# Cross-attention of a six-layer block on Trainium2: a new hand-written order for the short-context loop

## What is computed

```python
xn  = layer_norm(x, gamma)
ctx = layer_norm(context, ctx_gamma)          # context: 16 x 1601 x 512
q = (xn @ Wq) in 16 heads of 64, times 64**-0.5
k, v = split(ctx @ Wkv)                       # one key head and one value head for all 16 query heads
sim = where(mask == 0, -inf, q @ k.T)
out = softmax(sim) @ v ; out = out @ Wout + silu(gate) * a @ Wff2
```

## Time and profile before

| | before |
|---|---|
| median of 3 runs | 1497.53 us |
| the profiled execution | 1495.54 us |
| its span, first to last instruction | 1493.7 us |
| mean granted TensorE clock | 0.954 of full speed |
| PE busy | 1287.0 us (86%) |
| DVE busy | 916.6 us (61%) |
| ACT busy | 585.0 us (39%) |
| POOL busy | 502.7 us (34%) |
| chain that ended last, by engine | PE 63%, DVE 22%, issue 5%, ACT 4%, DMA 2% |

### The profile page before, as it was taken

How to read it: one execution, slowest core, us unless ns; L and a number is a source line. 1 busy time by engine, 2 the same in 40 slices (tenths; PEclk the granted TensorE clock), 3 DMA queues, 4 the chain that set the end, 5 groups by cost and what they waited for, 6 DMA issues and landing times.

```text
span 1493.7 us, 29148 instructions
## 1 busy us (share of the span) xinstructions
PE 1287.0 (86%) x11410; PEld 734.2 (49%) x11518; DVE 916.6 (61%) x2053; ACT 585.0 (39%) x1165; POOL 502.7 (34%) x424
## 2 busy tenths in 40 slices
PE   6857777787879999999998787989897998879998
PEld 2435555555664444444444445444444455555554
DVE  7768877776673333300367777485998366575761
ACT  3535676777763222231032416142314234233430
POOL 3002200000009555444225410054690039996300
PEclk9978999999999999999999997999999999769999
DMA  6223233221102211463100100031320001110000
GB/s 186 70 82 111 73 102 105 84 64 39 46 2 85 84 57 43 97 197 100 57 29 16 44 30 29 12 101 58 113 92 29 1 1 59 58 58 1 1 22 36
DMA packets 57474, 92.37 MB, mean 62 GB/s; under 512 B 14449, under 2 KB 14961, under 8 KB 57345
## 3 DMA queue, kind: packets, MB, share of 16 engines
q1 hardware_dynamic: 49728, 75.55, 16.3%
q10 hardware_dynamic: 5696, 8.76, 2.0%
q0 software_dynamic: 1920, 6.29, 1.3%
HBM read 88.49 MB, written 2.10 MB: 61 GB/s over the span
## 4 chain that ended last, share of the span: by engine, by line
PE 63%; DVE 22%; issue 5%; ACT 4%; DMA 2%; DVEq 0%; ACTq 0%; SPq 0%
PE psum L669 41%; PE psum L999 7%; PE psum L1323 4%; DVE big L2299 3%; DVE big L2305 2%; PE psum L678 2%; DMA ybuf<-in_ctx_dram 2%; PE psum L905 1%; DVE big L2280 1%; PE psum L1011 1%; DVE stats L2241 1%; PE psum L1311 1%; ACT big L1445 1%; PE psum L923 1%; DVE big L2512 1%
## 5 line engine op out<-in xcount | busy, mean ns | idle before, releaser
L3076 POOL TENSOR_TENSOR ring_hi<-stage,small 128x512 bf16<-128x512 f32 x128 | 140.8, 1100 | 635.0 <-DVE big L2324 396.8
L669 PE MATMUL psum<-y_mem,ring_hi 128*128 128x512 bf16 x867 | 263.3, 383 | 9.3 <-issue 4.3
L669 PE MATMUL psum<-ring_hi,y_mem 128*128 128x512 bf16 x551 | 168.2, 391 | 6.2 <-DVE ring_lo L2638 3.3
L669 PE MATMUL psum<-y_mem,ring_lo 128*128 128x512 bf16 x440 | 168.4, 383 | 0.3
L3079 POOL TENSOR_TENSOR ring_lo<-stage,ring_hi 128x512 bf16<-128x512 f32 x128 | 154.5, 1207 | 10.0
L669 PEld LDWEIGHTS psum<-y_mem,ring_hi 128*128 (+1 forms) x896 | 87.0, 99 | 108.9 <-issue 10.0
L1445 ACT ACTIVATE big<-psum 100x512 bf16<-100x512 f32 (+3 forms) x208 | 112.0, 554 | 55.5 <-PE psum L678 45.7
L669 PE MATMUL psum<-ring_lo,y_mem 128*128 128x512 bf16 x347 | 117.0, 390 | 3.6 <-issue 1.7
L669 PEld LDWEIGHTS psum<-ring_hi,y_mem 128*128 128x128 bf16 x576 | 57.5, 100 | 74.4 <-issue 11.9
L2305 DVE TENSOR_TENSOR big<-psum,big 100x512 bf16<-100x512 f32 x128 | 87.0, 680 | 8.2 <-ACT big L1445 6.9
L2409 DVE TENSOR_TENSOR side<-psum,ybuf 128x512 f32<-128x512 f32 x32 | 22.1, 691 | 110.3 <-ACT ybuf L1672 110.3
(11 more groups left out here) (273 smaller groups left out, 2783.8 us busy)
## 6 DMA issues: line engine op xcount, KB each, us to landing
ybuf<-in_ctx_dram SPq DMA_DIRECT2D x64, 200.0 KB
big<-in_ctx_dram SPq DMA_DIRECT2D x64, 200.0 KB
stage<-in_L_xattn_Wff_dram SPq DMA_DIRECT2D x12, 1024.0 KB, 5.4
ybuf<-in_L_ffn_W_fc_dram ACTq DMA_DIRECT2D x16, 256.0 KB, 2.8
ybuf<-in_L_ffn_W_proj_dram ACTq DMA_DIRECT2D x16, 256.0 KB, 2.8
stage<-in_L_ffn_W_fc_dram SPq DMA_DIRECT2D x4, 1024.0 KB, 5.2
stage<-in_L_ffn_W_proj_dram SPq DMA_DIRECT2D x4, 1024.0 KB, 5.1
stage<-in_L_xattn_Wout_dram SPq DMA_DIRECT2D x3, 1024.0 KB, 5.2
```

The source lines that it names most:

```text
L669: ins = pe.matmul(bank, l, r, start=n == 0, stop=n == len(passes) - 1)
L3076: pool.tensor_tensor(hi[:, k], src[:, k], zero, ALU.add).then_inc(pool_part, 1)
```

## The change

Nothing that is computed changes. Four things move.

1. **Value products two steps behind.** `values(g - 2)` in place of `values(g - 1)` stands after `turn_p(g)` on PE.
2. **Keys and values in pieces.** The 12 key matmuls are issued as 6 + 3 + 3 in steps j = 3 and 4, the 48 value matmuls as 12 + 12 + 24 within step j = 5, and the value matmuls move from step 6 to step 5. Three context tiles are transposed a batch earlier, in steps 6 and 7 of batch b for batch b + 2, the fourth in step 0.
3. **Consumers later.** On DVE `keys_low` moves from the head of step 5 to the tail of step 4, behind `low_p`; `out_low` from step 3 to the tail of step 2; `out_normed` behind `low_p` of step 0; `ctx_low` follows its tiles. ACT's `mask_rows` moves from step 1 to step 3 and its `ctx_normed` to steps 1, 3 and 5.
4. **Early statistics.** SP loads the first 16 context tiles right behind the short vectors, 4 to their own place and 12 to nine spare slots; DVE takes 8 of these statistics during queries 4 to 7 and 8 during queries 8 to 15. The roots of batches 0 and 1 come before the branch. 48 tiles are left for the steps of batches 0 to 8. The idle products ahead of the first context transpose fall from 24 to 8.

```diff
-        STAT_GROUPS = ((0, 1), (1, 2), (2, 4), (4, 8), (8, 12), (12, 16))
+        STAT_GROUPS = ((0, 2), (2, 4), (4, 6), (6, 9), (9, 12), (12, 16))
-        newton_at = {0: 2, 2: 3, 6: 4, 10: 5}
+        newton_at = {1: 2, 3: 3, 6: 4, 9: 5}
+        EARLY = 4 * TAIL_TILES
+        stats_in = {0: (0, 8), 1: (1, 7), 2: (1, 7), 3: (2, 6), 4: (2, 6), 5: (2, 6), 6: (1, 6), 7: (1, 6), 8: (1, 7)}
...
-                        idle_products(psum[:, 6, :], 24)
+                        idle_products(psum[:, 6, :], 8)
...
                     if g + 2 < STEPS:
                         scores(g + 2)
+                    if j == 3 and b + 1 < B:
+                        keys(b + 1, 0)
+                        keys(b + 1, 1)
+                    if j == 5 and b + 1 < B:
+                        values_of_keys(b + 1, 0)
                     turn_p(g)
-                    if g:
-                        values(g - 1)
-                    if j < 4 and b + 1 < B:
-                        turn_ctx(b + 1, j)
+                    if j == 5 and b + 1 < B:
+                        values_of_keys(b + 1, 1)
+                    if g >= 2:
+                        values(g - 2)
+                    if j == 0 and b + 1 < B:
+                        turn_ctx(b + 1, 3)
...
+                    if j == 3 and b + 1 < B:
+                        keys(b + 1, 2)
                     if j == 4 and b + 1 < B:
-                        keys(b + 1)
-                    if j == 6 and b + 1 < B:
-                        values_of_keys(b + 1)
+                        keys(b + 1, 3)
+                    if j == 5 and b + 1 < B:
+                        values_of_keys(b + 1, 2)
+                        values_of_keys(b + 1, 3)
+                    if j == 6 and b + 2 < B:
+                        turn_ctx(b + 2, 0)
+                    if j == 7 and b + 2 < B:
+                        turn_ctx(b + 2, 1)
+                        turn_ctx(b + 2, 2)
...
                 query(n)
+                if n >= 4:
+                    tile_stats()
+                    tile_stats()
+            run(inverse_roots(0))
...
-            stage_block(2)
-            stage_block(3)
+            for t in range(TAIL_TILES):
+                sp.dma_start(xmap(TAIL_TILES)["ctx"][0:TAIL_ROWS, t], tail_rows(t)).then_inc(ctx_in[t], 16)
+            for t in range(TAIL_TILES, EARLY):
+                i = (t - TAIL_TILES) % len(early_slots)
+                if t == TAIL_TILES + 4:
+                    stage_block(2)
+                if t == EARLY - 3:
+                    stage_block(3)
+                if t >= TAIL_TILES + len(early_slots):
+                    sp.wait_ge(stat_used, t - len(early_slots) + 1)
+                sp.dma_start(early_slots[i][0:TAIL_ROWS], tail_rows(t)).then_inc(early_in[i], 16)
```

More of the change, by code:

```diff
@@ L935, in attend_short @@
                 query(13)
-                keys(0)
+                for k in range(KC):
+                    keys(0, k)
                 query(14)
-                values_of_keys(0)
+                for u in range(TAIL_TILES):
+                    values_of_keys(0, u)
                 query(15)
@@ L943, in attend_short @@
                 pe.wait_ge(q_lo, 16)
+                for kt in range(3):
+                    turn_ctx(1, kt)
                 for g in range(STEPS):
@@ new lines, in inverse_roots @@
+            def inverse_roots(q):
+                t0, t1 = (4 * b for b in STAT_GROUPS[q])
+                x, y, t = (tail["nw"][0:R, i, t0:t1] for i in range(3))
+                mean, var = (tail["mv"][0:R, t0:t1, i] for i in range(2))
+                due()
+                later(dve.tensor_scalar(x, var, LN_EPS, None, ALU.add))
+                yield
+                due()
+                later(dve.tensor_scalar(y.bitcast(I32), x.bitcast(I32), 1, None, ALU.arith_shift_right))
+                yield
+                due()
+                dve.tensor_scalar(x, x, -0.5, None, ALU.mult)
+                later(dve.tensor_scalar(y.bitcast(I32), y.bitcast(I32), -1.0, RSQRT_SEED, ALU.mult, ALU.add))
+                yield
+                for _ in range(3):
+                    due()
+                    later(dve.tensor_tensor(t, y, y, ALU.mult))
+                    yield
+                    due()
+                    later(dve.tensor_tensor(t, t, x, ALU.mult))
+                    yield
+                    due()
+                    later(dve.scalar_tensor_tensor(out=y, in0=t, scalar=1.5, in1=y, op0=ALU.add, op1=ALU.mult))
+                    yield
+                due()
+                dve.scalar_tensor_tensor(out=x, in0=mean, scalar=-1.0, in1=y, op0=ALU.mult, op1=ALU.mult).then_inc(rstd_ready, 1)
+                yield
@@ L2224, in attend_short @@
                 n_keys = TAIL_TILES * R
[L2225 to L2274, removed]
                 def ctx_low(b, kt):
@@ L2352, in attend_short @@
                 maximum(0)
-                for _ in range(2):
-                    tile_stats()
+                roots = inverse_roots(1)
+                some(roots, 4)
                 maximum(1)
-                run(inverse_roots(1))
+                ctx_low(1, 0)
+                sums = iter(())
                 for g in range(STEPS):
                     b, j = divmod(g, 8)
[L2359 to L2363, removed]
+                    if j == 0 and b in newton_at:
+                        roots = inverse_roots(newton_at[b])
@@ L2364, in attend_short @@
                     if g + 2 < STEPS:
                         maximum(g + 2)
-                    if j == 7:
+                    some(roots, 1 if b else 4)
+                    if j == 0 and b + 1 < B:
+                        ctx_low(b + 1, 1)
+                        ctx_low(b + 1, 2)
+                    if j == 1 and b + 1 < B:
+                        ctx_low(b + 1, 3)
+                    if b in stats_in and stats_in[b][0] <= j < stats_in[b][1]:
+                        tile_stats()
+                    if j == 6:
+                        if b + 1 < B:
+                            values_low(b + 1)
@@ L2367, in attend_short @@
                         sums = inverse_sums(b)
                         some(sums, 1)
-                    if b or j > 1:
-                        some(roots, 2)
+                    if j == 7:
+                        some(sums, 1)
+                        if b + 2 < B:
+                            ctx_low(b + 2, 0)
+                    low_p(g)
+                    some(roots, 1)
                     if j == 0 and b:
                         out_normed(b - 1)
-                    if 1 <= j <= 4 and b + 1 < B:
-                        ctx_low(b + 1, j - 1)
@@ L2375, in attend_short @@
-                    if j == 3 and b:
+                    if j == 2 and b:
                         out_low(b - 1)
[L2377 to L2380, removed]
-                        some(roots, 2 if b else 5)
-                    for _ in range(stat_at.count((b, j))):
-                        tile_stats()
-                    if j == 3:
-                        run(roots)
-                    low_p(g)
@@ L2387, in attend_short @@
-                    run(sums)
+                    if j == 4 and b + 1 < B:
+                        keys_low(b + 1)
+                    if j == 6:
+                        some(sums, 1)
+                    if j == 7:
+                        run(sums)
                 assert taken[0] == TAIL_TILES * B
@@ L2393, in _ @@
             with dve.If(head_rows_used > 0):
+                for i in range(len(early_slots)):
+                    dve.wait_ge(early_in[i], 16 * ((EARLY - TAIL_TILES - 1 - i) // len(early_slots) + 1))
                 for n in range(8, 16):
```

180 lines of the change are left out of this document (113 added, 67 removed).

## The result

The changed kernel takes 1403.22 us (median of 4 runs, 1399.6 to 1407.3): 0.9379 of before, interval 0.9346 to 0.9412, a gain of 94 us. The profiled execution took 1399.60 us (before 1495.54).

The account below looks back on a forecast made before the run. No engine was full (DVE idle 78.7 of 313.37 us), so the order sets the time. Batches 1 to 15 -48.3, batch 0 -15.4, query stage +1.2, clock +2: -60.5 us, to 1437 us from the median; range 1419 to 1466.

Parts of the forecast that it names:

- The long stretch: Batches 1 to 15, first to last `out_normed`: 313.37 us falls to 265.1, a gain of 48.3 us.
- the sizes named as signs: Marks of a right forecast, among them a stretch of 250 to 280 us and first `maximum` within 3 us of 89.88.
- the "best" bound of -61.7: Batches 1 to 15: the largest gain allowed, 61.7 us, with 15 us of DVE idle time left.
- Batch 0: First `maximum` to first `out_normed`, 43.39 us before: falls to 28.0 with no load on the chain, a gain of 15.4 us.
- The allowance for scatter: Batches 9 to 14: 1.1 us added to the hand-worked time of each batch, giving 16.4 us and 2.4 us DVE idle.
- The bare walk: One batch without statistics followed through the new order, nothing added: the next batch starts at 15.3 us.
- the slower rival: Attention steps: PE at its lower clock doubles its 14.7 us per batch to 29.4; +128 us, 1613 us; chance 0.04.
- the 4.8 us for a slot: Statistics loads in batch 0: 3.8 us landing, 0.3 issue, 0.7 statistics; under two steps of 2.8 to 3, so hidden.
- The query stage and the clock: Before the first `maximum`: added DVE work loses 1.2 us, PE's lower clock level after idling another 2 us.
- Lock-step: Batches 1 to 15: each step lasts as long as its slowest engine; stretch 294 us, 1466 us in all; chance 0.20.
- the start alone: Only batch 0 gains; waits move to `copy_p` and `out_normed`, later batches stay at 20.9 us; 1485 us; chance 0.06.
- The clock rival: Attention steps: PE at its lower clock level makes the stretch 441 us against 313; 1613 us in all; chance 0.04.

## Why the prediction was wrong

**The long stretch failed, in both of its DVE terms.** I wrote 234.7 + 2 + 28.4 = 265.1 us: busy time as it was, the added roots, and idle time. Measured: 225.5 busy and 236.44 - 225.51 = 10.9 idle. Of the 28.7 us missed, 11.2 are busy time and 17.5 idle time. The mechanism held: `keys_low`'s wait is gone, `maximum`'s is 1.3 us, no load stands on batch 0's chain, the clock is above 0.95, and `low_p` waits for `copy_p` 21 times only. What failed are two of the sizes named as signs: the stretch lies below 250 us, and the first `maximum` came 4.9 us late, not within 3.

*Busy time was taken for fixed work.* Five kernels do nearly the same DVE work in the stretch (634 to 643 instructions); its busy time falls with the idle time:

| kernel | stretch | DVE busy | DVE idle |
|---|---|---|---|
| before | 313.37 | 234.68 | 78.7 |
| before, values two behind | 294.81 | 232.76 | 62.1 |
| changed, values one behind | 268.62 | 231.83 | 36.8 |
| changed, pieces undone | 245.85 | 227.11 | 18.7 |
| changed | 236.44 | 225.51 | 10.9 |

An instruction with another right behind it is overlapped by that one: `low_p` lasts 0.68 us, the next starts 0.60 after it. An instruction that a wait follows has no such overlap: before, 57 of the stretch's 120 `low_p` had a successor that began within their record, after, 109 of 119. Added up singly, DVE's instructions of the stretch last 274.5 us before and 273.0 after; the busy time counts the overlaps once, and these grew from 39.8 to 47.5 us. An estimate from the trace of before, each kind of instruction at its time from start to start where the next one follows closely, is 221 us. So 234.7 was no floor, and the "best" bound of -61.7 was none either.

*Some work stood in the sum twice.* Batch 0 was given the `ctx_low` and the `low_p` that the new order brings into it, but 234.7 still held them. The stretch has 53 `ctx_low` and 119 `low_p` after, 56 and 120 before: about 2 of the 11.2 us.

*The allowance for scatter was too large.* I gave batches 1 to 8 1.0 us of idle time each, 9 to 14 2.4 each, the last 6: 8 + 14.4 + 6. Measured: 0.7, 8.4 and 1.8. The bare walk (15.3 us per batch) was nearer to 14.95 than the walk with its allowance (16.4). It also named the wrong engine. ACT's 15.2 per batch was a right reading of the old order (15.15 in the exact batch below, where DVE has 13.67, not 14.0), but busy time behind waits again:

```profile
374.53:395.08 20.55, 16.41 (x227) 12.34 (x226) 13.67 (x36) 15.15 (x37) 0.00 (x0) 1.00 0.15 41
```

```profile
273.43:288.37 14.94, 14.94 (x226) 12.52 (x225) 13.43 (x36) 14.79 (x37) 0.00 (x0) 1.00 0.20 58
```

The second row is batch 10 in the changed kernel: ACT is busy for nearly as long as PE, but the chain of batches 10 to 13 is PE alone. Its 14.94 us are near the 14.7 that I had added up from instructions for the slower rival.

**Batch 0 held**: -17.1 for -15.4, no load on its chain, and the loads, one per step, held DVE for 0.2 us. The 3.8 us per load were luck: the earlier trace rows is not of these loads. Its landings are those of 24 gathers that POOL issues from the same tensor at 967 to 1077 us; the trace has no landing for SP's loads. It has the six that stood on batch 0's chain before, 2.9 to 3.7 us each (start, us), among them:

```profile
97.36 3.70 DMA ybuf<-in_ctx_dram
...
102.50 2.93 DMA ybuf<-in_ctx_dram
```

So the 4.8 us for a slot came out near enough, and the longest landing of 5.7 us is no figure of these loads.

**The query stage and the clock**: +4.9 for +1.2 and +2. Query 13 starts 77.89 - 75.47 = 2.4 us later than before, because two `ctx_low` stood behind a query and a statistic on DVE, as the walk had it; at the lower clock level it took 5.09 - 2.60 = 2.5 us more. I had sized the first term at half.

**Behind the attention**: -6.8 in the profiled execution, where I had 0. The same kernel again took 1402.38 - 357.15 = 1045.2 us there, so 3 us of it are scatter between executions. A stage 850 us behind the last `out_normed` ran at a clock of 0.62 before and 0.74 after:

```profile
1296.64:1336.64 40.00, 28.46 (x635) 22.74 (x635) 32.25 (x66) 13.23 (x18) 38.68 (x28) 0.62 0.25 77
```

```profile
1207.50:1247.50 40.00, 29.72 (x578) 22.77 (x578) 31.77 (x67) 15.24 (x23) 38.88 (x28) 0.74 0.24 79
```

In the same kernel again this stage ran at 0.74 too, with 3 us more behind the attention, so its clock does not explain the time alone. The profiled executions of the other orders took 1043.8 to 1047.5 us there, all below 1048.90: whether a part goes with the change stays open.

**The rivals.** Lock-step (294 us; its eight step times add up to 18.3, not 18.4, which moves it by 1.5) and the start alone (313) are out at 236. The clock rival is out: 1.00 through the stretch, a third of whose TensorE work is transposes. The Trainium skill (TensorE: Matmul & The Clock Gate, Part 4) does not count transposes as busy for the clock in the way of products. As two thirds of the work are products, these 236 us neither bear that out nor speak against it, and nor do the 22 us of the earlier trace rows.

## What to carry to other kernels

When a change removes waits, add up the work of each engine from start to start of instructions that follow closely, per batch, and take the largest; busy time read behind waits is too long (here 234.7 us against an estimate of 221). A walk that already had every wait needed little on top here. Look at which instructions a row of landings belongs to before you price a load by it. Undo parts one at a time from the finished order too, not only add them to the old one: what a part gives depends on whether the next obstacle is gone.

## What the runs showed of the hardware

DVE's busy time for nearly the same work fell by 9.2 us as its idle time fell by 67.8, because records of instructions that follow closely overlap (0.68 us long, the next after 0.60). And loads asked for early enough cost nothing with two slots: twelve 200 KB tiles, one of them read without a wait 3.57 us after it was asked for, did not hold DVE once in the query stage.
